# Attention with keys ordered by the block transpose and queries left in dealt row order, with the hand-over to the feed-forward half reordered

## The reference

```
x = x + tanh(g1) * attention(layernorm(x), ctx)      # 16 heads of 32 columns, 128 queries, 128 keys
x = x + tanh(g2) * ffn(layernorm(x))                 # square(relu(h @ up)) @ down, plus a routed expert, layernorm
attention: q = rms_norm(xn @ wq + bq); k = rms_norm(ctx @ wk + bk); v = ctx @ wv + bv
           out = (softmax(q k^T / sqrt(32)) v) @ wo + bo
```

## Time and profile before

| | |
|---|---|
| median of 3 runs | 1385.67 us (1385.57 to 1386.1) |
| the profiled execution | 1383.14 us, its span 1381.0 us |
| mean granted clock of PE | 0.995 |
| PE busy | 1346.0 us (97%) |
| DVE, ACT, POOL busy | 955.8 (69%), 584.6 (42%), 515.7 (37%) us |

### The profile page before, as it was taken

One profiled execution on the slowest core, in us unless ns is written; L12 is line 12 of the kernel. 1 busy time (PEld: TensorE's weight loads), 2 busy tenths in 40 slices (PEclk: granted clock), 3 DMA queues, 4 the chain that ended last, 5 costly groups with the idle time before them and its releaser, 6 DMA issues.

```text
span 1381.0 us, 27851 instructions
## 1 busy us (share of the span) xinstructions
PE 1346.0 (97%) x8924; PEld 1133.2 (82%) x8924; DVE 955.8 (69%) x1824; ACT 584.6 (42%) x1835; POOL 515.7 (37%) x671
## 2 busy tenths in 40 slices
PE   6999999999999999899999999999999999999996
PEld 5777777777777777788888898888898988888984
DVE  5666666666666765788686786775775785776764
ACT  4777777777766667532312312212222213123210
POOL 3565566666556765443022131131140240140121
PEclk9999999999999999999999999999999999999998
DMA  6377777777777762356648549449458368367541
GB/s 230 99 196 205 204 206 202 206 203 207 205 186 176 196 157 70 112 194 167 215 137 205 177 140 255 145 150 251 130 156 260 128 169 252 118 176 220 171 142 39
DMA packets 402771, 243.71 MB, mean 176 GB/s; under 512 B 303121, under 2 KB 303249, under 8 KB 402705
## 3 DMA queue, kind: packets, MB, share of 16 engines
q1 hardware_dynamic: 370448, 184.15, 49.3%
q10 hardware_dynamic: 32256, 58.73, 12.6%
HBM read 178.60 MB, written 64.23 MB: 176 GB/s over the span
## 4 chain that ended last, share of the span: by engine, by line
PE 85%; issue 6%; DVE 4%; ACT 2%; POOL 1%; DMA 1%; ACTq 0%; SPq 0%; POOLq 0%; DVEq 0%
PE bank L76 17%; PE bank L78 16%; PE bank L77 16%; PE wide L77 7%; PE wide L78 7%; PE wide L76 7%; PE bank L417 4%; PE wide L396 4%; PE bank L408 4%; ACT prob L787 1%; DMA prob<-in_wk 1%; PE wide L1664 1%; PE wide L1661 1%; PE wide L1672 1%; DVE c L1471 0%
## 5 line engine op out<-in xcount | busy, mean ns | idle before, releaser
L1738 ACT ACTIVATE hT_hi<-c 128x512 fp32r<-128x512 f32 x128 | 79.9, 631 | 403.8 <-PE wide L78 206.3
L1970 POOL TENSOR_TENSOR pair<-pair,beta 128x512 f32<-128x512 f32 x28 | 37.3, 1334 | 449.7 <-DMA pair<-x_scratch 449.7
L77 PE MATMUL wide<-wo_lo,hT_hi 128*128 128x512 f32 x512 | 203.2, 397 | 0.0
L78 PE MATMUL wide<-wo_hi,hT_lo 128*128 128x512 f32 x512 | 202.0, 395 | 0.0
L76 PE MATMUL wide<-wo_hi,hT_hi 128*128 128x512 f32 x512 | 201.6, 394 | 0.0
L787 ACT ACTIVATE prob<-wide,nmx 128x128 f32<-128x128 f32 x512 | 182.0, 410 | 2.3 <-DVE nmx L599 2.3
L963 POOL TENSOR_TENSOR prob<-prob,rr 128x512 f32<-128x512 f32 x128 | 133.1, 1040 | 125.4 <-DVE rr L607 125.4
L1816 DVE TENSOR_TENSOR hT_lo<-c,hT_hi 128x512 fp32r<-128x512 f32 x128 | 99.8, 799 | 75.1 <-ACT hT_hi L1738 74.8
L787 ACT ACTIVATION_READ_ACCUMULATOR prob<-wide,nmx 128x1 f32 x512 | 128.6, 251 | 0.0
L78 PEld LDWEIGHTS wide<-wo_hi,hT_lo 128*128 128x128 f32 x512 | 96.1, 188 | 22.7
L76 PEld LDWEIGHTS wide<-wo_hi,hT_hi 128*128 128x128 f32 x512 | 96.2, 188 | 21.8 <-DMA wo_lo<-ring_scratch 0.3
(11 more groups left out here) (234 smaller groups left out, 3551.6 us busy)
## 6 DMA issues: line engine op xcount, KB each, us to landing
wo_hi<-ring_scratch ACTq DMA_DIRECT2D x110, 256.0 KB, 3.6
wo_lo<-ring_scratch ACTq DMA_DIRECT2D x110, 256.0 KB, 4.4
wo_hi<-ring_scratch SPq DMA_DIRECT2D x46, 256.0 KB, 2.7
wo_lo<-ring_scratch SPq DMA_DIRECT2D x46, 256.0 KB, 3.0
fx<-x_scratch SPq DMA_DIRECT2D x36, 256.0 KB
xin<-in_x SPq DMA_DIRECT2D x32, 256.0 KB, 3.3
cin<-in_ctxT SPq DMA_DIRECT2D x32, 256.0 KB, 3.1
xres<-in_x SPq DMA_DIRECT2D x32, 256.0 KB, 4.3
```

The costliest lines, as they stand in the source:

```text
L77: eng.matmul(dst, ah, bl, start=False, stop=False)
L78: mm = eng.matmul(dst, al, bh, start=False, stop=last and k == n - 1)
L1738: return act.activation(dst, src, ACT.Copy)
```

## The change

- kT is written by the block transpose with the keys in another order inside each head group (`turn_k` with the order "p (k b c) -> p c k b"), so that the scores read it in plain order. Each run of the transpose is now written with a step of 4 elements (16 bytes), where it was contiguous.
- The values read pT in plain order, so queries stay in dealt row order for all batches. The load of xres and the store of x2 take the DRAM rows in that order instead (`in_rows`): 16 x 8 rows for batches 1 to 30, 4 x 32 rows for batch 31, as they are for batch 0. For direct batches 1 and 2 ACT writes qT with a step of 8 elements (only for batch 2 before).
- In slots 29 and 30 the splits of the gate and the first up weights stand ahead of the evictions of the probabilities on ACT and ahead of the maxima on DVE.
- In slot 31 the output projection of batch 30 goes to another bank and behind `ff.turn(2)`, the wait for its eviction stands later, and ACT and DVE take some steps in another order; `ff.turn(2)` writes bank 5 instead of 4.

```diff
-            def by_key(a):
-
-                return a.rearrange("p (c b) -> p b c", c=KT)
-
-            def by_query(b, a):
-
-                if isinstance(b, int) and b < XD - 1:
+            def in_rows(b, a):
+
+                if is_slot(b, 0):
                     return a
                 if is_slot(b, NB - 1):
-                    return a.rearrange("p (c b) -> p b c", c=KT)
-                return a.rearrange("p (h l) -> p l h", l=8)
+                    return a.rearrange("(b c) d -> c b d", c=KT)
+                return a.rearrange("(l h) d -> h l d", l=8)
...
-                        load(a, 1 - par, t["x"], xres, ld_r)
+                        sp.dma_start(xres[1 - par][:, :], in_rows(a, t["x"][a])).then_inc(ld_r[1 - par], DMA)
...
-                        sp.dma_start(x2_dram[o], x2[par][:, :]).then_inc(st_x2[par], DMA)
+                        sp.dma_start(in_rows(o, x2_dram[o]), x2[par][:, :]).then_inc(st_x2[par], DMA)
...
-                        keys = by_key(cols(kT, h)) if kq_dealt(s) else cols(kT, h)
                         for g in range(NG):
-                            mm = pe.matmul(cols(bank[g], h), cols(qT, h)[strip(g), :], keys[strip(g)], start=True, stop=True)
+                            mm = pe.matmul(cols(bank[g], h), cols(qT, h)[strip(g), :], cols(kT, h)[strip(g)], start=True, stop=True)
...
-                            mm = pe.matmul(dst[strip(h), :], cols(vb[par], g)[:, strip(h)], by_query(a, cols(pT[:, g, :], h)),
-                                           start=True, stop=True)
+                            mm = pe.matmul(dst[strip(h), :], cols(vb[par], g)[:, strip(h)], cols(pT[:, g, :], h), start=True, stop=True)
...
                     values(a, a % 2)
-                    project_out(a, BO)
                     ff.turn(pe, 2, t_first)
+                    project_out(a, BO_NEXT)
...
-                    pe.wait_ge(dv_x2, a + 1)
                     ff.turn(pe, 5, t_first)
...
                     ff.turn(pe, 7, t_first)
+                    pe.wait_ge(dv_x2, a + 1)
                     ff.upward(pe, 0, 0)
...
-                    turn_blocks(kT, k_dealt).then_inc(dv_kT, 1)
+                    turn_blocks(kT, k_dealt, "p (k b c) -> p c k b").then_inc(dv_kT, 1)
...
+                    if is_slot(s, NB - 3):
+                        ff.split_gate_lo(dve)
+                    if is_slot(s, NB - 2):
+                        for m in range(3):
+                            ff.up_lo(dve, 0, m)
                     maxima(s, 0)
...
                 def drain(s, a, o):
+                    inverse(a, 3)
                     residual_sum(o, o % 2, BO)
                     take_probs(a, 1)
-                    inverse(a, 3)
...
-                    ff.lo_T(dve, 0, 0)
                     maxima(s, 2)
                     split_values(a)
+                    ff.lo_T(dve, 0, 0)
...
-                    if is_slot(n, XD - 1):
+                    if is_slot(n, 1) or is_slot(n, 2):
                         dst = dst.rearrange("p (k h l) -> p k l h", k=KT, l=8)
...
+                    if is_slot(s, NB - 3):
+                        ff.split_gate_hi(act)
+                    if is_slot(s, NB - 2):
+                        act.wait_ge(pe_K, NB)
+                        for m in range(3):
+                            ff.up_hi(act, 0, m)
                     take_probs(a, 0)
...
                     exps(s, s % 2, 0)
+                    hi_aT(a)
                     ff.hi_T(act, 0, 0)
-                    hi_aT(a)
...
-    T_BANK = (6, 7, 4, 6, 7, 5, 7, 7)
+    T_BANK = (6, 7, 5, 6, 7, 5, 7, 7)
```

More of the change, by code:

```diff
@@ L150, in flamingo_layer @@
             BTP_LAST = [bank[n] for n in (1, 2, 3, 1)]
-            BO_LAST = bank[3]
+            BO_NEXT, BO_LAST = bank[4], bank[3]
             t_first = [sb(ctx, f"tsum{n}", [P, D]) for n in range(4)]
@@ L346, in drain @@
                     sp.wait_ge(dv_x2, a - 1)
-                    load(a, a % 2, t["x"], xres, ld_r)
+                    sp.dma_start(xres[a % 2][:, :], in_rows(a, t["x"][a])).then_inc(ld_r[a % 2], DMA)
                     sp.wait_ge(dv_x2, o + 1)
-                    sp.dma_start(x2_dram[o], x2[o % 2][:, :]).then_inc(st_x2[o % 2], DMA)
-                    load(s, s % 2, t["x"], xres, ld_r)
+                    sp.dma_start(in_rows(o, x2_dram[o]), x2[o % 2][:, :]).then_inc(st_x2[o % 2], DMA)
+                    sp.dma_start(xres[s % 2][:, :], in_rows(s, t["x"][s])).then_inc(ld_r[s % 2], DMA)
                     for m in range(GB, GB + 2):
@@ L353, in drain @@
                     sp.wait_ge(dv_x2, a + 1)
-                    sp.dma_start(x2_dram[a], x2[a % 2][:, :]).then_inc(st_x2[a % 2], DMA)
+                    sp.dma_start(in_rows(a, x2_dram[a]), x2[a % 2][:, :]).then_inc(st_x2[a % 2], DMA)
                     for m in range(GB + 2, 2 * GB):
@@ L357, in drain @@
                     sp.wait_ge(dv_x2, s + 1)
-                    sp.dma_start(x2_dram[s], x2[s % 2][:, :]).then_inc(st_x2[s % 2], DMA)
+                    sp.dma_start(in_rows(s, x2_dram[s]), x2[s % 2][:, :]).then_inc(st_x2[s % 2], DMA)
                 run(sp, slot, before, drain)
@@ L575, in lo_xT, with turn_blocks @@
                         sub(xnT_lo[:, :], BTX, xnT_hi[:, :]).then_inc(dv_xT, 1)
-                def turn_blocks(dst, src):
-                    return dve.transpose(runs(dst, "p (k c b) -> p c k b"), runs(src, "p (c k b) -> p c k b"))
+                def turn_blocks(dst, src, order="p (k c b) -> p c k b"):
+                    return dve.transpose(runs(dst, order), runs(src, "p (c k b) -> p c k b"))
                 def turn_x(b):
@@ L735, in drain @@
                     inverse(s, 2)
-                    residual_sum(a, a % 2, BO)
+                    residual_sum(a, a % 2, BO_NEXT)
                     ff.lo_T(dve, 0, 2)
@@ L902, in slot @@
                         hi_xT(n + 1)
[L903 to L907, removed]
                 def drain(s, a, o):
```

4 lines of the change are left out of this document (removed).

## The result

| | before | after |
|---|---|---|
| median of 4 runs each | 1385.88 us (1385.57 to 1386.4) | 1361.68 us (1359.1 to 1365.02) |
| the profiled execution, its span | 1383.14, 1381.0 | 1365.02, 1362.9 |

The ratio is 0.9826 (95% interval 0.9805 to 0.9848): 24.2 us faster. The forecast was 1332 (1327 to 1343), so the side was right and the size was not: 29.7 us of the gain did not come. The page of after answers to the earlier trace rows; its second line is the chain's share by engine, which was 85% PE before.

What follows compares the result with a forecast made beforehand. PE was taken as the bound, busy 1346.0 of 1381.0 us. Terms -51.8 - 1.9 - 2.1 + 2.4 = -53.4 from 1383.1 gave 1329.7; with 2.5 for the median, 1332 us (range 1327 to 1343).

Steps and rivals of the forecast that it cites:

- The small matmuls: Attention slots 3 to 30 on PE: plain-order scores save 24.6 us and values 27.2, together 51.8 us.
- The loop through DRAM: Slots with halves: q_dealt's late landing delays the K bias, costing 0.12 us in each of 20 slots, 2.4 us.
- Rival 1: The loop through DRAM sets the period: 0.5 us in 20 slots, 10 us instead of 2.4, giving 1340; chance 0.23.
- the prediction's own sign of being wrong: Middle attention slots: a slot over 15.5 us, or ACT's evictions releasing the values late in most, would refute the forecast.
- The new write of kT: DVE's strided block transpose takes 1.4 us against 0.7, hidden by 1.6 us of slack; price nothing.
- The rows of x and of the sums: Rearranged loads and stores: batch 31's store may take 2.8 us instead of 0.7; price 0, bounds 0 to 1.
- Rival 2: Rearranged tiles run on 4 DMA engines in every slot, period 17.5 us, about 1398 in all; chance 0.03.
- The hand-over: End of attention: reordering removes PE's waits of 1.23 and 0.86 us, saving 2.1, beyond the values' 1.9.
- ACT's wait for the values and the K bias: Steady slots: ACT's wait of up to 2.0 us shrinks to 0.15; the K bias waits behind q_dealt, not PE.

Runs made afterwards that it cites:

- turnq_late: The changed kernel with DVE's turn of q moved behind the next batch's K bias and normalisation: 1336.22 us.
- scores_only: The kernel before with only kT written in the new order and scores read in plain order; values, rows and hand-over as before: 1361.86 us.
- both_moves: The changed kernel with DVE's turn of q behind the K bias and normalisation, and SP's q_dealt issue ahead of the halves: 1336.64 us.
- old_handover: both_moves with slots 29 to 31 in the order of the kernel before: 1340.25 us.
- ctx_late: The changed kernel with POOL's lo part of the context behind the root for q instead of ahead of it: 1357.14 us.
- plain_rows: both_moves with batch 31's store and the first four feed-forward tile loads in plain row order, not the reference's: 1331.07 us.

## Why the prediction was right or wrong

**The small matmuls: right.** 1.10 and 1.01 us where PE is the bound. With the loop cut PE's busy time is 52.1 us less, as 51.8 were priced, and turnq_late brings 49.1 of the whole 53.4.

**The loop through DRAM: the step that failed.** The prediction anchored q_dealt's issue "8.48 us into the slot (SP is held there by the order of its queue, not by PE)" and k_dealt's at +5.15, and took the rest from there. SP is indeed held by the order of its queue, but the queue stands behind the deal of k, that behind kf, kf behind the root, the root behind the K bias and that behind qT, which waits for the last slot's q_dealt. Nothing in this is tied to the start of the slot. Before, kf began at +0.65 of the slot (300.56 - 299.91); in the slot of after that begins at 296.26 it begins at +2.72, k_dealt is issued at +7.99 and q_dealt at +10.96. I priced a late landing by what it costs the evictions once, 0.12 us, when a lateness that comes back to itself has to be summed around the loop: 15.72 us in the turn shown, 16.4 on average, against the 15.05 that PE would need. The price should have been 1.35 us a slot.

Rival 1 had the idea, and at 0.23 too small a chance, but looked for it on the side of x and the deal of q and priced it at 0.5 us a slot; the prediction's own sign of being wrong (over 15.5 us in a middle slot) came true in 19 of the 20. What made the loop longer than the durations of before gave is above all kf: 0.95 to 1.71 us, a term that had no line in the working at all. With the means of before for kf with its issue (0.99), the deal of k (3.50 and 0.11 to the next issue), SP's five issues (3.03) and q_dealt's landing (4.37), and the steps behind the landing without slack as after has them (3.16), one turn adds up to 15.2 us; after has 16.3 by the same count. So the sum would have told beforehand that the loop ties with PE's 15.05, but not by how much it would pass it: 0.84 of the 1.1 us between are kf's, 0.24 the landing's.

**The new write of kT: right in kind, high in size.** 1.10 us where 1.4 was taken. DVE's wait for k_dealt ahead of it is 20.7 us. That the slack hides the extra 0.4 us is shown by scores_only. Both the strided read on PE and this strided write pay, which agrees with the rule of the Trainium skill (Advanced Engine Details and Errata, SBUF Cachelines) that the prediction weighed.

**The rows of x and of the sums: wrong by 2.2 us for batch 31,** taken as 0 with bounds of 0 and 1, and by 3.9 with the slow stretch that came behind the wait. It was placed behind PE's last projection and gate; in fact the ring's loads queue behind it and the first down product waits. The rule of the Trainium skill (DMA: Bandwidth & Descriptors, Why a DMA increments its semaphore by 16 and not by 1) said 16 engines for batches 1 to 30 and 4 for batch 31. The times agree, though no row here counts engines: slots of 15.05 with the patterns of 16 in each, and stalls that leave with the outer count of 4. Rival 2 falls with this. The prediction did not ask which transfers of the kernel before have that outer count already: the first feed-forward loads, 2.8 us in slots 24 and 25.

**The hand-over: about right.** 3.5 us with the values' share in the trace of after and 4.1 in that of both_moves, where 4.0 were priced. The reordering alone was priced at 2.1; old_handover shows 3.0 in the trace and 3.6 by the medians.

**ACT's wait for the values and the K bias: right.** The first is gone (1.2 us in all), and the bias no longer waits for PE, as foreseen. That the bias would wait for q_dealt was foreseen too; only what follows from it was not carried around the loop.

## What to carry to other kernels

Where a change makes the bound engine faster, list the loops that lead from one iteration to the next without passing that engine (over DRAM and an issuing queue above all), add up their whole length from rows, and compare it with the new period. Where the two come within a few tenths of a microsecond, as 15.2 and 15.05 here, anything that stretches a member of the loop is paid in full in every turn. A wait inside such a loop can be near zero in the old trace and each one short in the new, and no single wait in the list shows the loss; the chain of waits does. If a loop is the bound, look for the place where program order ties two independent chains together (here qT ahead of the K bias) before shortening any transfer: moving two lines gave as much as the whole change did.

## What the runs showed of the hardware that was not expected

- **A DVE operation stretched by POOL.** kf takes 0.75 us alone (ctx_late) and 1.75 when it starts just behind POOL's 1.27 us subtraction; in the slot above POOL runs from 298.91 to 300.18 and kf from 298.98 to 300.73. In every slot of before and of after in which kf starts during this subtraction (29 and 28) it ends 0.55 us behind POOL's end, however early it started: before, it started 0.8 to 1.0 us into the subtraction in all slots but one and so took 0.81 to 1.01. The Trainium skill (SBUF — State Buffer, SBUF: two separate sides) says that DVE and POOL share one pair of ports as an exclusive lock, also for a DVE operation with two SBUF inputs against a POOL operation that reads SBUF; kf has two, the subtraction reads SBUF, and the trace agrees.
- **A transfer with an outer count of 4 holds up issues behind it.** An ordinary load's issue took 3.59 and 3.35 us in SP's queue, and 3.27 and 4.61 in turnq_late, in the slots behind two such loads each. With four transfers of 32 rows in their place it took 1.75 and 1.84, and neither slot stalled. Long issues are not theirs alone: in plain_rows, without any, the longest took 2.67.
- **A short wait of PE can cost twice.** 2.24 us of idling at the ring was followed by a stretch at a granted clock of 0.50 in four of seven traces, with 1.6 us more for 24 matmuls (7.41 against 5.76).
- **Queue order shows in the landing.** q_dealt lands in 2.9 us in the median when issued ahead of three 256 KB transfers, in 4.6 behind them.
- **Strided block transpose on DVE**: 1.10 us against 0.70 for 128x512 f32 with a step of 16 bytes in the written operand, less than ACT's 1.25 against 0.58 for a step of 32 bytes.
